# Attention and triangular inverse as one matrix per system in a five-stage ViT kernel on one core

## The chip, the cores and the metric

One core of a Trainium2 chip runs the whole forward pass in one launch. The metric is device microseconds of that core from start to end, the median of three runs. Engines: TensorE (PE; PEld is its weight load), VectorE (DVE), ScalarE (ACT), GpSimd (POOL), and SyncE (SP), which issues DMAs.

## The reference

Input is 64 images of 3 x 96 x 96; each becomes TOK = 37 tokens of D = 256. Five stages follow, each added to its input: embedding, 16-head attention with shared keys, a gated mixture of low rank (MuMoE), a delta-rule attention with two heads of 128, and a top-1 expert network with 8 experts. The change is in the fourth. For 37 tokens there is one chunk and a zero starting state, so per image and head it comes to:

```python
k = x / max(norm(x), 1e-12)                    # x: normalised rows, per head
v = (x @ W_write.T) * beta                     # beta = sigmoid(x @ W_beta.T)
A0 = tril(-((k * beta) @ k.T * L), -1)         # L[i, j] = gamma ** (i - j), i >= j
A = solve_triangular(eye - A0, eye, lower=True, unit_diagonal=True)
attn = tril(k @ k.T * L)
o = attn @ (A @ v)
return out + o @ W_read.T                      # both heads side by side
```

## The kernel before

All data is f32. Three images make a tile of R = 111 rows; there are NT = 22 tiles, PAIRS = 11 pairs of them. The work is in phases with barriers: embedding and first attention (to about 280 us), the gates, and a third phase (from 306 us) with MuMoE, the delta-rule attention, the router and the experts. Each engine runs its own list of instructions strictly in order, ordered among engines by semaphores with waits written by hand (`wait_ge`; `free(eng, sem, n)` waits for a buffer).

**Pair loop** (i from -1 to PAIRS + 1, about 306 to 455 us). Per pair: MuMoE, layer norm to `xn`, transposes to `xk`, then per tile `row_products` on TensorE (values and beta logits to bank 6, the Gram matrix of each head to bank 7). VectorE's `decay_products` makes two 111x222 products of the Gram matrix: with `lt` to `attn_t` (decayed lower part, transposed, kept for all tiles) and with `ln` to `nf`. GpSimd does `power_rows` (which the loop's next normalisation waits for), `add_rows` (h += xn), `inverses` (1/norm from the squares), `strengths` (four small operations per tile: beta, beta/norm, beta/norm^2, and beta/norm spread over the image mask) and `fold` (three images' blocks side by side to 37 columns per head, times the strength: rows of N). SP stores these rows to `n_rows` in DRAM.

**Solve.** Systems are regrouped, one system (image, head) per partition. Three GROUPS of pairs: 0 (tiles 0-9), 1 (10-15), 2 (16-21, LAST). SP's `load_systems(g)` brings N of a group; VectorE's `substitution(g)` solves for columns of the inverse X, two rows per step, as a generator: `advance(budget)` runs some steps in slots between VectorE's other work, by estimated costs. A group has SETS of partitions that share the columns, so X has 703, 481 and 370 values per partition in groups 0, 1 and 2. `identity_columns(g)` writes the identity there first. At the end an `engine_nop` signals `solved[g]`; SP's `store_inverses(g)` and `load_inverses(g)` bring X back by rows, in a round trip through DRAM.

**Tile loop** (t from 2 to NT + 4, about 455 to 531 us). A software pipeline; per turn:

- TensorE: `solve_values(t)` (ab x values, two heads), `read_out(t-1)` (each head to its own half of a bank), `turn_outputs(t-5)` (two transposes), `attend(t)`, `router_logits(t-5)`.
- ScalarE: `normalise_outputs(t-4)`, `copy_solved(t)`, `copy_turned(t-5)`, `scale_first(t-1)` (first head's read-out times 1/norm, to `first_half`), `copy_attended(t)`.
- VectorE: `add_read(t-2)` (second head's read-out times 1/norm, added to h; statistics; variance + EPS), `keep_logits(t-5)`, then `advance(1.1)`. Before tile 10 and tile 16 it must finish the substitution of their group (`advance(math.inf, ...)`).
- GpSimd (its own t from 0): `add_first(t-1)` (h += first_half), `spread_inverses(t+2)` (inverse blocks to the 111x222 matrix `ab`), `power_outputs(t-2)` (1/std).

Then `route` counts tokens per expert on VectorE, with placing matmuls on TensorE (L1011) and filler matmuls before and behind them (`keep_busy`, L992 to 995). After that come 26 tiles of 128 rows through their experts. SP loads `in_w` in three parts (L1343, L1346, L998); the last waits for all stores of `x_rows`.

## Time and profile before

| | us |
|---|---|
| median of three runs | 780.35 |
| the three runs | 780.12, 780.35, 784.51 |
| the profiled execution | 781.44 |
| its span, first to last instruction | 779.7 |

| engine | busy us | share |
|---|---|---|
| TensorE | 672.8 | 86% |
| its weight loads | 512.7 | 66% |
| VectorE | 419.7 | 54% |
| GpSimd | 292.6 | 38% |
| ScalarE | 246.8 | 32% |

Busy is the time inside instructions, not the rate at which they work. Shares are means over stages with different limits; the stage from about 430 to 560 us is the one in which TensorE has holes. A granted clock of 1.00 is TensorE's full clock (2.4 GHz), 0.50 its lower one (1.2 GHz). "Idle before <- X" in a row means that the engine had nothing to do until X finished.

### The profile page before, as it was taken

The page shows a single profiled execution, that of the slowest core. Times are in us where ns is not written, and L with a number is a line of the kernel's source. Part 1 is how long each engine was busy: PE and PEld are TensorE (multiplying, and loading weights), DVE is VectorE, ACT ScalarE, POOL GpSimd, SP SyncE. Part 2 cuts the span into 40 slices and gives each one's busy share as a digit, 9 for nine tenths or more (in the row PEclk, how much of TensorE's full clock was granted, in tenths as well). Part 3 has the DMA queues.
Part 4 walks back from the last instruction along what each step waited for, and adds up shares of the span by engine and source line. Part 5 has one row for each costly group of instructions (what it writes and reads, how often), then busy time and mean ns, then how long its engine had stood idle before and what let it go on. Part 6 is the DMA issues. An engine that isn't in the chain of part 4 may idle for free.

```text
span 779.7 us, 13703 instructions
## 1 busy us (share of the span) xinstructions
PE 672.8 (86%) x4576; PEld 512.7 (66%) x4576; DVE 419.7 (54%) x1120; ACT 246.8 (32%) x679; POOL 292.6 (38%) x483
## 2 busy tenths in 40 slices
PE   5899999999997614999999589495999999999994
PEld 3566776676765413899999567373667676676763
DVE  2456677777665475244389999557233333333331
ACT  0123333333333114344444256261032323222231
POOL 2344544544444100165566777360222222223220
PEclk9899999999998755899999999896799999999998
DMA  8311001111100000000011216698101111211110
GB/s 302 123 36 32 24 21 34 37 36 37 37 2 1 1 0 2 1 6 8 22 24 32 43 45 236 254 362 309 54 28 55 44 59 41 62 41 51 53 34 14
DMA packets 25070, 50.73 MB, mean 65 GB/s; under 512 B 15611, under 2 KB 15741, under 8 KB 24363
## 3 DMA queue, kind: packets, MB, share of 16 engines
q1 hardware_dynamic: 21387, 35.36, 14.1%
q0 software_dynamic: 3328, 10.23, 4.3%
q10 hardware_dynamic: 288, 4.27, 1.3%
q8 instruction: 39, 0.64, 0.3%
q14 instruction: 28, 0.23, 0.1%
HBM read 39.99 MB, written 9.86 MB: 64 GB/s over the span
## 4 chain that ended last, share of the span: by engine, by line
PE 45%; DVE 7%; issue 4%; POOL 3%; ACT 0%; POOLq 0%; DVEq 0%; ACTq 0%
PE psum L1192 12%; PE psum L1168 11%; PE psum L1389 5%; PE psum L1401 4%; PE psum L1181 3%; PE psum L1435 2%; DVE work L1741 1%; PE psum L1369 1%; PE psum L1011 1%; DVE arena_w L1748 1%; PE psum L1379 1%; POOL work L1900 1%; PE psum L1411 1%; PE psum L1441 1%; POOL work L1889 1%
## 5 line engine op out<-in xcount | busy, mean ns | idle before, releaser
L1265 ACT ACTIVATE work<-psum,cst 128x128 f32<-128x128 f32 x208 | 56.6, 383 | 144.1 <-PE psum L1181 144.1
L1168 PE MATMUL psum<-arena_w,work 128*128 x208 | 93.7, 593 | 1.3 <-DVE work L1219 1.3
L1192 PE MATMUL psum<-arena_w,work 128*128 x416 | 94.2, 379 | 0.4 <-ACT work L1265 0.4
L1130 POOL DMA_INDIRECT out<-work,row_i x26 | 25.8, 990 | 158.0 <-DVE work L1241 158.0
L1192 PEld LDWEIGHTS psum<-arena_w,work 128*128 128x128 f32 x416 | 77.1, 190 | 10.5 <-issue 1.1
L1228 DVE COPY work<-psum 128x512 f32<-128x512 f32 x52 | 36.0, 692 | 67.7 <-PE psum L1168 57.4
L347 PE MATMUL psum<-arena_w 128*111 128x256 f32 x264 | 64.3, 397 | 4.9 <-DMA arena_w<-in_pack 4.9
L712 POOL TENSOR_TENSOR arena_w<-arena_w,work 101x592 f32<-101x592 f32 x33 | 39.6, 1200 | 71.8 <-DVE work L578 71.8
L1168 PEld LDWEIGHTS psum<-arena_w,work 128*128 128x128 f32 x208 | 37.5, 190 | 38.8 <-issue 38.8
L347 PEld LDWEIGHTS psum<-arena_w 128*111 128x111 f32 x264 | 46.8, 183 | 19.6 <-issue 9.6
L703 POOL TENSOR_TENSOR arena_w<-arena_w 128x296 f32<-128x296 f32 x66 | 44.0, 690 | 20.7 <-DVE arena_w L546 20.7
L1235 DVE TENSOR_TENSOR tokens<-psum,cst 128x256 f32<-128x256 f32 x26 | 11.1, 425 | 73.9 <-PE psum L1192 73.9
L401 PE MATMUL psum<-arena_w 128*37 128x296 f32 x264 | 41.2, 434 | 3.3 <-ACT arena_w L666 3.3
L635 ACT COPY arena_w<-psum 37x592 f32<-37x592 f32 x33 | 25.2, 765 | 57.8 <-PE psum L412 57.8
L1389 PE MATMUL psum<-arena_w 128*128 128x222 f32 x176 | 40.9, 379 | 0.5 <-DVE arena_w L1642 0.5
L1123 POOL DMA_INDIRECT tokens<-x_rows,row_i x26 | 25.5, 980 | 34.1 <-DVE gate_s L1086 26.5
L558 DVE TENSOR_REDUCE work<-psum 101x16 f32<-101x592 f32 x33 | 25.4, 771 | 23.8 <-PE psum L401 23.8
L1389 PEld LDWEIGHTS psum<-arena_w 128*128 128x128 f32 x176 | 34.3, 202 | 5.1 <-issue 3.0
L412 PEld LDWEIGHTS psum<-cst,arena_w 101*128 101x128 f32 x264 | 26.5, 149 | 16.6 <-POOL arena_w L712 9.0
L433 PE MATMUL psum<-arena_w 37*32 37x74 f32 x1056 | 24.5, 230 | 13.6 <-DVE arena_w L569 12.1
L1401 PE MATMUL psum<-arena_w 128*128 128x222 f32 x176 | 35.8, 356 | 0.0
L627 ACT ACTIVATE arena_w<-arena_w 101x592 f32<-101x592 f32 x33 | 23.5, 711 | 37.4 <-DVE arena_w L561 36.4
(220 smaller groups left out, 1332.4 us busy)
## 6 DMA issues: line engine op xcount, KB each, us to landing
arena_w<-in_w SPq DMA_DIRECT2D x2, 4096.0 KB, 13.6
arena_w<-in_x SPq DMA_DIRECT2D x22, 333.0 KB, 3.0
x_rows<-tokens SPq DMA_DIRECT2D x22, 192.0 KB, 5.2
arena_w<-in_pack ACTq DMA_DIRECT2D x1, 2442.0 KB, 9.2
cst<-in_packc ACTq DMA_DIRECT2D x1, 1727.0 KB, 13.4
arena_w<-in_pack SPq DMA_DIRECT2D x1, 818.5 KB, 7.0
arena_w<-in_pack SPq DMA_DIRECT2D x2, 384.0 KB, 4.3
arena_w<-n_rows SPq DMA_DIRECT2D x8, 85.6 KB, 2.8
```

Source lines behind the costliest of these rows:

```text
L347: mm = nc.tensor.matmul(bank[0][0:R, j * D:(j + 1) * D], xp[j][:, k * R:(k + 1) * R], w_lin[:, k, :], start=(k == 0), stop=(k == PC - 1))
L401: mm = nc.tensor.matmul(bank[4 + f][e * HP:e * HP + TOK, 0:HH * TOK], qt[:, a:a + TOK], kb[p % 2 * 2 + e], start=True, stop=True)
L412: mm = nc.tensor.transpose(turns_bank[:, c * 128:c * 128 + PR], prob[p % 2][:, c * 128:(c + 1) * 128], ident[0:PR, 0:PR])
L703: nc.gpsimd.tensor_tensor(kb[p % 2 * 2 + e].rearrange("p (h s) -> p h s", h=HH), kt[:, a:a + TOK].unsqueeze(1).broadcast_to([128, HH, TOK] ...
L712: nc.gpsimd.tensor_tensor(by_head(prob[p % 2], HP), by_head(prob[p % 2], HP), small[p % 2][:, 2 * NH:3 * NH].unsqueeze(2).broadcast_to([PR ...
L1130: pool.indirect_dma_start(out_h, bass.IndirectOffsetOnAxis(ap=row_i[:, 2 * i + j:2 * i + j + 1], axis=0), yo[j], None).then_inc(y_stored[j ...
L1168: mm = nc.tensor.matmul(bank[2 * j + f][:, :], xgt[j][:, k * 128:(k + 1) * 128], arena_w1[:, bass.ds(expert * (2 * FF) + (k * FF + f * 512 ...
L1192: mm = nc.tensor.matmul(bank[7][:, 0:D], ht[j][:, g * 128:(g + 1) * 128], arena_w2[:, bass.ds(expert * (FC * D) + g * D, D)], start=(g == ...
L1228: nc.vector.tensor_copy(hp[j][:, f * 512:(f + 1) * 512], bank[2 * j + f][:, :]).then_inc(h_out[j], 1)
L1265: nc.scalar.activation(ht[j][:, g * 128:(g + 1) * 128], bank[4 + f][:, k * 128:(k + 1) * 128], ACT.Gelu, bias=cst[:, bass.ds(expert * FC + ...
L1389: mm = nc.tensor.matmul(bank[2 + f // 2 % 2][:, (f % 2) * W:(f % 2 + 1) * W], w_out1[:, f, :], z1, start=True, stop=True)
L1401: mm = nc.tensor.matmul(bank[1][:, 0:W], w_in2[:, f, :], hid[:, f * W:(f + 1) * W], start=(f == 0), stop=(f == OC - 1))
```

## The change

With M = I - A0, A = M^-1, B = diag(beta) and D the diagonal of k k^T, attn = D + B^-1 (M - I), because M's part below the diagonal is beta times that of attn. Hence attn A B = D A B + I - B^-1 A B: below the diagonal entry (i, j) is A[i, j] times a factor of row i and one of column j, and the diagonal has a factor of its own. Applied to X in the solver's layout, one elementwise product gives the matrix that maps values to outputs. In the code:

- `attn_t`, `lt`, and their set-up (two ScalarE exponentials, two GpSimd products, two constants) go; `decay_products` makes one product.
- Rows of N are stored without strength, and grow from 37 to NW = 40 columns: the three further ones carry strength, the diagonal's correction and 1/norm. `factors(i)` on GpSimd computes these for a pair in ten small operations, in place of `strengths`; `fold` has two operations. A store of N now waits for `factors_ready` too. GpSimd's order in the pair loop changes: `fold(i-2, 0)`, `power_rows`, (`scale_columns`), `factors`, `add_rows`, `fold(i-2, 1)`, ..., (`last_factors`).
- In the solver's layout GpSimd scales N's columns (`scale_columns(g)`: a copy of 37 values, products of 324 and 648 values per partition) and builds the factor matrix F (`last_factors(g)`: two operations of X's size). `substitution(g)` waits for `scaled[g]` instead of the load, and ends with a product X F of X's size instead of the nop. For group 2 the two stand in GpSimd's tile loop, at t = 2 behind `spread_inverses(4)` and ahead of `power_outputs(0)`, and at t = 4.
- `identity_columns` writes two matrices, at i = 0, 1, 2 of the pair loop. Group 2 has room of its own, so its load no longer waits for `z1_done`.
- `solve_values`, `copy_solved`, `scale_first`, `add_first` go. `attend` multiplies the values with the new `ab` (norm factors in place of beta/norm) into banks 0 and 1; `read_out` sums both heads in one bank (2 or 3); transposes and logits use banks 4 and 5. `add_read` is one addition; + EPS moves to GpSimd's `power_outputs`. `keep_logits` moves to ScalarE as a copy; b_r is added once in `route`.
- Orders in a turn: TensorE `attend(t)`, `turn_outputs(t-5)`, `read_out(t-1)`, `router_logits(t-5)`; ScalarE `copy_attended(t)`, `copy_turned(t-5)`, `normalise_outputs(t-4)`, `keep_logits(t-5)`.
- `keep_busy` before the placing goes from 4 to 5 calls, over five banks.

```diff
@@ store_systems
                     sp.wait_ge(nk_ready, t + 1)
+                    sp.wait_ge(factors_ready, 3 * (t // 2 + 1))
@@ route_products, route
-                keep_busy(pe, 4)
+                keep_busy(pe, 5)
...
+                link(tt(by_tile(lgr), by_tile(lgr), c("b_r", R).unsqueeze(1).broadcast_to([R, NT, NE]), ALU.add))
@@ TensorE
-                def solve_values(t):
...
                 def attend(t):
...
-                    pe.wait_ge(vn_out, t + 1)
+                    pe.wait_ge(a_block, t + 1)
                     free(pe, o_out, t - 1)
                     for h in range(H1):
-                        a = (t * H1 + h) * R
-                        mm = nc.tensor.matmul(bank[2 + t % 2][:, h * R:(h + 1) * R], vn[t % 2][:, h * 128:(h + 1) * 128],
-                                              attn_t[:, a:a + R], start=True, stop=True)
+                        mm = nc.tensor.matmul(bank[t % 2][:, h * R:(h + 1) * R], x_half(t)[:, h * 128:(h + 1) * 128],
+                                              ab[t % 2][:, h * R:(h + 1) * R], start=True, stop=True)
...
-                        mm = nc.tensor.matmul(bank[4 + t % 2][0:R, h * D:(h + 1) * D], ot[t % 2][:, h * R:(h + 1) * R],
-                                              w_read[:, h, :], start=True, stop=True)
+                        mm = nc.tensor.matmul(bank[2 + t % 2][0:R, 0:D], ot[t % 2][:, h * R:(h + 1) * R],
+                                              w_read[:, h, :], start=(h == 0), stop=(h == H1 - 1))
...
                 for t in range(2, NT + 5):
-                    solve_values(t)
+                    attend(t)
+                    turn_outputs(t - 5)
                     read_out(t - 1)
-                    turn_outputs(t - 5)
-                    attend(t)
                     router_logits(t - 5)
@@ VectorE
-                    nc.vector.tensor_tensor(attn_t[:, t * H1 * R:(t + 1) * H1 * R], bank[7][0:R, 0:H1 * R], lt, ALU.mult)
...
-                    dve.wait_ge(n_in[g], 16 * H1 * sets)
+                    dve.wait_ge(scaled[g], 2)
...
-                    nc.vector.engine_nop().then_inc(solved[g], 1)
+                    dve.wait_ge(factored[g], 2)
+                    nc.vector.tensor_tensor(rows_x[0:used, :], rows_x[0:used, :], rows_f[0:used, :], ALU.mult).then_inc(solved[g], 1)
...
-                    nc.vector.scalar_tensor_tensor(h, bank[4 + j][0:R, D:2 * D], inv_all[:, t * H1 + 1:t * H1 + 2], h,
-                                                   ALU.mult, ALU.add).then_inc(added, 1)
+                    nc.vector.tensor_tensor(h, h, bank[2 + j][0:R, 0:D], ALU.add).then_inc(added, 1)
@@ GpSimd
+                def scale_columns(g):
...
+                    pool.wait_ge(n_in[g], 16 * H1 * SETS[g])
+                    ts(col_s[g][0:used, :], n[:, :, TOK], 1.0, None, ALU.mult).then_inc(col_ready[g], 1)
+                    pool.wait_ge(col_ready[g], 1)
+                    half = TOK // 2
+                    for r0, r1 in ((1, half + 1), (half + 1, TOK)):
+                        part = n[:, r0:r1, 0:r1 - 1]
+                        tt(part, part, col_s[g][0:used, 0:r1 - 1].unsqueeze(1).broadcast_to([used, r1 - r0, r1 - 1]),
+                           ALU.mult).then_inc(scaled[g], 1)
+
+                def last_factors(g):
...
+                    pool.wait_ge(zeroed[g], 2)
+                    for k, op in ((TOK + 2, ALU.mult), (TOK + 1, ALU.add)):
+                        tt(to, to, n[:, :, k].unsqueeze(1).broadcast_to(shape), op).then_inc(factored[g], 1)
...
                 for t in range(NT + 2):
-                    add_first(t - 1)
                     spread_inverses(t + 2)
+                    if t == 2:
+                        scale_columns(LAST)
                     power_outputs(t - 2)
+                    if t == 4:
+                        last_factors(LAST)
```

## Rows read from the trace of the kernel before

**Rows 1.** Stretches of the span: length, busy us (instructions) per engine, granted clock, DMA

```profile
390.00:410.00 20.00, 20.00 (x113) 18.26 (x112) 17.34 (x50) 9.72 (x35) 13.95 (x34) 1.00 0.10 22
430.00:450.00 20.00, 12.03 (x60) 10.01 (x59) 19.11 (x57) 6.16 (x27) 13.49 (x30) 0.86 0.29 40
480.00:490.00 10.00, 10.00 (x72) 8.48 (x70) 9.59 (x41) 7.03 (x20) 8.47 (x16) 1.00 1.07 461
```

**Rows 2.** Waits of SP's queue, 430 to 560 us: total, times, longest

```profile
SPq L1318 <- DVEq L1754: 35.7, 3, 21.3
```

**Rows 3.** Timeline of SP: start us, us, instruction

```profile
458.06 4.59 SPq L1300 DMA_DIRECT2D arena_w<-n_rows  x8
...
497.78 3.67 SPq L1318 DMA_DIRECT2D a_rows<-arena_w  x8
502.80 2.66 SPq L1324 DMA_DIRECT2D arena_w<-a_rows  x6
...
534.73 0.35 SPq L998 DMA_DIRECT2D arena_w<-in_w  x1
```

**Rows 4.** Timeline of TensorE, restart at tile 16 and one tile of the drain

```profile
505.59 1.20 PE L1450 MATMUL psum<-tokens,work 111*111 111x128 f32 x4 [11.11 <-POOL work L1889]
...
509.74 0.67 PE L1450 MATMUL psum<-tokens,work 111*111 111x128 f32 x4
...
517.45 0.67 PE L1450 MATMUL psum<-tokens,work 111*111 111x128 f32 x4
517.96 1.03 PE L1471 MATMUL psum<-cst,work 128*111 128x256 f32 x4
518.83 0.36 PE L1484 MATMUL psum<-cst,tokens 111*128 111x111 f32 x2
519.02 0.61 PE L1461 MATMUL psum<-arena_w,work 111*128 111x111 f32 x4
519.62 0.56 PE L1493 MATMUL psum<-cst,work 128*111 128x8 f32 x4
```

**Rows 5.** Timeline of VectorE

```profile
444.02 1.03 DVE L1741 TENSOR_TENSOR work<-arena_w 108x130 f32<-108x130 f32 x1
...
445.40 0.39 DVE L1741 TENSOR_TENSOR work<-arena_w 108x150 f32<-108x150 f32 x1
...
469.95 0.48 DVE L1775 SCALAR_TENSOR_TENSOR tokens<-psum,arena_w,tokens 111x256 f32<-111x256 f32 x1
...
493.58 0.47 DVE L1775 SCALAR_TENSOR_TENSOR tokens<-psum,arena_w,tokens 111x256 f32<-111x256 f32 x1
...
531.38 0.34 DVE L1027 TENSOR_REDUCE work<-work 111x22 f32<-111x176 f32 x1
```

**Rows 6.** Groups by line and form: count, busy us, mean ns of one, idle before

```profile
L1846 POOL TENSOR_TENSOR tokens<-tokens,arena_w 111x512 f32<-111x512 f32 x11 | 13.5, 1228 | 0.9 <-DVE arena_w L1678 0.9
L1864 POOL TENSOR_TENSOR arena_w<-arena_w 111x2 f32<-111x2 f32 x22 | 4.6, 208 | 1.8
L1698 DVE TENSOR_TENSOR arena_w<-cst,arena_w 120x703 f32<-120x703 f32 x1 | 0.9, 893 | 1.1 <-PEq L179 1.1
L1235 DVE TENSOR_TENSOR tokens<-psum,cst 128x256 f32<-128x256 f32 x26 | 11.1, 425 | 73.9 <-PE psum L1192 73.9
L1588 ACT COPY work<-psum 128x222 f32<-128x222 f32 x22 | 7.5, 343 | 17.0 <-PE psum L1484 17.0
```

**Rows 7.** Timeline of GpSimd, the first `power_outputs`

```profile
459.46 0.83 POOL L1900 TENSOR_TENSOR work<-work 111x1 f32<-111x1 f32 x1
```

**Rows 8.** Stretches and TensorE's timeline around the router's placing matmuls

```profile
542.00:544.00 2.00, 0.00 (x0) 0.00 (x0) 1.97 (x4) 0.00 (x0) 0.00 (x0) 0.86 1.18 508
544.00:546.00 2.00, 1.71 (x8) 1.71 (x9) 2.00 (x5) 0.00 (x0) 0.00 (x0) 0.50 0.64 279
...
535.26 5.96 PE L995 MATMUL psum<-cst 128*128 128x512 f32 x8
544.29 9.63 PE L1011 MATMUL psum<-tokens 111*128 111x52 f32 x44 [3.07 <-DVE tokens L1075]
```

## Blind prediction

> **What bounds the kernel now.** I read the table of stretches first, then the waits of the sync engine's queue (SP), then the timelines of SP, TensorE, VectorE and GpSimd from 430 to 560 us. Until about 430 us TensorE is busy in every microsecond at the full clock, 2.4 GHz [rows 1]: the third phase's pair loop is TensorE's, and what the change takes from VectorE or adds to GpSimd there is covered, as long as neither falls behind. From 430 us TensorE has holes. What is then waited for is the triangular solve on VectorE: SP waited 35.7 us, in three waits, for the end of a substitution before it could send the inverses away [rows 2]. The third (group 2) ends at about 497.7, its inverses are issued from 497.78, read back from 502.80 [rows 3], and TensorE, idle for 11.1 us, restarts at 505.59 [rows 4]. From there to the router's first instruction at 531.38 [rows 5] the last tiles drain at TensorE's rate, 2.57 us per tile [rows 4]. So the change pays in two places: (a) when substitution 2 ends, (b) how long the drain lasts. The expert stage behind is untouched.
>
> **(a) The end of substitution 2.** *In the loop.* Each tile loses the 111x222 product for attn_t; the neighbouring one on VectorE is of its form, and I count 0.3 us, two per pair, covered by TensorE until pair 10. `strengths` (4 small GpSimd operations per tile) becomes `factors` (10 per pair), `fold` loses one operation. A small one costs 0.21 us and about 0.07 of handover [rows 6], so GpSimd's work per pair is 14 operations before and after. Order matters more: at i = 11 the eight-operation difference falls badly, since all ten of `factors` (2.8 us at most, 2.4 by my count, as some are not chained) now stand before `add_rows` and `spread_inverses(0)`, where four stood: +1.4, minus 0.4 for `fold`, so a_block(0) comes 1.0 us later. `attend(0)` is ahead of `row_products(10, ...)` on TensorE, so the last rows of N move by that 1.0. At i = 12 `factors(10)` stands before `fold(10, 1)` again, and the store of tile 20 now waits for `factors_ready`, so its two DMAs come right before tile 21's: +0.5. The load of group 2, issued from 458.06 to 462.65 [rows 3], moves by 1.5.
>
> *New in front of the substitution.* `scale_columns(2)` on GpSimd: a strided copy of 37 values, a product of 324 and one of 648. GpSimd takes 1.23 us for 512 in two inputs [rows 6], so 0.3 + 0.8 + 1.4 = 2.5 us. The last load ends its issue at 462.65 + 1.5; with 1.6 us to land, my allowance, and the 2.5 that gives about 468.2. VectorE comes there itself at: before, add_read(4) was at 469.95 after 1.9 us of substitution setup, so setup began near 468.0 [rows 5]. Now VectorE is 1.1 us later into this stretch, has the product of X and F of group 1 (481 values, 0.65 us; 703 cost 0.89 [rows 6]) more to do, and is about 0.26 us shorter in each of four `add_read`s: 468.6. The two meet; the scaling costs nothing in itself here, but 2.5 us if VectorE had been early.
>
> *What waits behind it.* GpSimd is in order: behind `scale_columns(2)` stand `power_outputs(0)`, which before ran at 459.46 [rows 7], and `spread_inverses(5)`. ScalarE's `normalise_outputs(0)` waits for the first, TensorE's `attend(5)` for the second. So the tile pipeline stops from tile 5 until about 470 us, TensorE idles some 8 us and restarts at the low clock (1.2 GHz), as it does after the hole before 505.59, where its four instructions of a solve take 1.20 us instead of 0.67 [rows 4]. Tile 4's `add_read` comes at about 473.3 where it was at 469.95 [rows 5]. VectorE is idle for those 3 us, since the substitution's next step stands behind that `add_read`. Two tiles more at a partly low clock, then VectorE sets the pace. Before, the nine tiles from `add_read(4)` to `add_read(13)` took 23.6 us [rows 5], 2.63 each, of which 1.33 was `add_read` with `keep_logits` and 1.30 substitution. Now the first is 1.07: the addition in 425 ns instead of 478 [rows 6], no EPS addition, no logits. Seven tiles gain 0.26 each, 1.8 in all, `add_read(13)` lands near 494.6, and the last steps plus the final product (0.5) end near 498.7: **+1.0 us**. Bounds: VectorE catches the stop up whole: -1.5; the stop is paid in full, from 459.46 to 468.2: +8.7.
>
> **(b) The drain.** The gaps between starts of one tile give TensorE's five parts [rows 4]: solve 0.51, read-out 0.87, turn 0.19, attend 0.60, logits 0.41. The solve goes; read-out keeps its two products, only accumulated. 2.57 becomes 2.06. Others per tile: ScalarE loses copy_solved and scale_first and gains a copy of 8 values, about 1.4 us; GpSimd loses `add_first` and gains a small operation, about 1.8; VectorE 1.07. All under 2.06. First tile at the low clock, 505.59 to 509.74 [rows 4]: 4.15 less its solve of 1.0: **-1.0**. Five more: 5 x 0.51 = **-2.55**. The rest, 509.74 + 5 x 2.57 = 522.6 to 531.38, is 8.8 us. Now: one iteration of 0.19 + 0.87 + 0.41 = 1.5, then four where only turn, a 0.34 us copy of 128x222 on ScalarE [rows 6] and logits alternate, 0.2 + 0.34 + 0.41 and three handovers, about 1.2 each, and 0.5 for the last logits and their copy: 6.9, **-1.9**. Sum **-5.4**; bounds -2.6 (only the five solves) and -7. The router gets b_r as one chained 111x176 addition: **+0.4**.
>
> **The router's filler.** `keep_busy` before the placing products goes from 4 to 5. Before, TensorE was idle from 541.2 to 544.29, the granted clock averaged 0.86 from 542 to 544 and was 0.50 after, so it fell shortly before the placing began; the 44 placing matmuls then ran at 0.50, 9.63 us for all [rows 8]. Four fillers took 5.96 us [rows 8], 1.5 each over both clocks; one more takes up to 1.5 us, about half of that if the clock has risen by then, so a quarter to half of that hole, so the clock may still be up when the placing starts. But those matmuls, 9.6 us without a hole, never raised it [rows 8]; I take them to lose it again soon. Bounds: 0 (clock already down) and half of 9.63, 4.8. I take nearer the first: **-1.3**. The last expert weights, issued 534.73 [rows 3], move with the issue of the stores, +1, and stay ahead of the experts' start near 560.
>
> **Sum.** +1.0 - 5.4 + 0.4 - 1.3 = -5.3 us. Against the profiled execution's own 781.44 (span 779.7, 1.7 around it) that is 776.1. That execution lay 1.1 above the median of 780.35; from the median it is 775.0.
>
> The locked port: VectorE's product of 130 values took 1.03 us beside GpSimd's 512-value addition, one of 150 alone 0.39 [rows 5]. The Trainium skill, "SBUF — State Buffer", section "Who interferes with whom", says that a VectorE operation with two SBUF inputs is shut out for a whole GpSimd instruction that reads SBUF, the exclusive lock going to whoever starts first. By that rule, which the row bears out, the new large GpSimd operations (three scalings, six factor products) speak against the change.
>
> **Rivals.**
> 1. *The placing keeps the full clock.* The shorter hole speaks for it, the 0.50 throughout the placing against. Price 4.8 instead of 1.3: **771.5**. Chance 0.17.
> 2. *The drain doesn't go at TensorE's pace.* ScalarE's `keep_logits` of one tile now stands before `copy_attended` of the next, so a ring TensorE-ScalarE-TensorE could hold 2.57. Then only the first tile and the drain gain, 2.9 instead of 5.4: **777.5**. ScalarE's idle share speaks against. Chance 0.12.
> 3. *The stop behind `scale_columns(2)` is paid in full* (slower). Place: GpSimd's third turn of the tile loop. 8.7 instead of 1.0: **782.7**. It decides once substitution 2 ends over 6.3 us later than before, 504. For it: GpSimd, ScalarE and TensorE stop together, and VectorE advances only behind an `add_read`. Against: VectorE's 0.26 per tile and TensorE's 0.51. Chance 0.12.
> 4. *Large GpSimd operations shut VectorE out*: each of `last_factors(2)` (370 values, 0.8 us twice) and four collisions of 0.6 us, as in rows 5, on VectorE's path in this stretch: +3.5: **778.5**. The Trainium skill's rule quoted above would have it so. Chance 0.12.
>
> **Chances.** The forecast 0.47, its own range 773 to 777.5. 775.0 is its time. The range 770.5 to 781 takes in rivals 1, 2 and 4. Within 1% (772.5 to 788.2) is about what a measurement of this kernel can't tell from no change: the forecast and rivals 2, 3 and 4 lie there, with an eighth of the forecast below it. Faster by over 1%: rival 1 and that eighth, 0.23. Slower by over 1% only if 3 and 4 join: 0.06. Same: 0.71.
>
> **What would show it.** The issue of group 2's inverses: 498.8 (was 497.78). VectorE idle about 3 us before tile 4's addition, and GpSimd waiting for the load of n_rows: the stop. Starts of one line on TensorE 2.06 us apart in the drain. From TensorE's restart to the router's first instruction 20.4 us (was 25.8). The granted clock in the placing: above 0.50 in its first microseconds. Wrong it goes if the issue comes later than 504, if the spacing stays at 2.57, or if the placing takes 5 us. The loop to 425 us should be the same to 0.5 us.

## Result: 2.5% slower, and the profile after

| | before | after |
|---|---|---|
| median of the paired runs | 781.21 us | 802.69 us |
| ratio, 95% interval | | 1.0253 [1.0213, 1.0293] |
| profiled execution (span, mean granted clock) | 781.44 (779.7, 0.925) | 802.33 (800.5, 0.900) |
| first power of the pair loop (GpSimd) | 324.48 | 322.59 |
| load of group 2 issued | 458.06 | 467.73 |
| inverses of group 2 stored | 497.78 | 511.45 |
| TensorE restarts at tile 16 | 505.59 | 521.04 |
| router's first instruction | 531.38 | 551.88 |
| placing begins | 544.29 | 565.17 |

Ratios leave out runs more than 1.5% above the fastest of their kernel; where single runs are told below, all of them are. The table splits the 20.5 us by which the router starts late: 13.7 up to the store of the last inverses, 1.8 more until TensorE restarts (9.6 us from store to restart, 7.8 before), and 5.0 in the drain, 30.8 us where it was 25.8. I had predicted +1.0 for the first and -5.4 for the last.

Positions in the span can't be compared more finely than by 4 us as they stand: in the twenty profiles of this document the pair loop's first power comes anywhere from 321.0 to 324.8 us, for kernels that are the same up to there too. Counted from that power, the last store is 15.6 us late after (188.9 us; before 173.3) and the load of group 2 11.6 us (145.1; 133.6). Where it matters, times below are counted so.

Of the 1.8 us between store and restart, the way of the inverses through DRAM has all: 6.9 us from the issue of the last store to that of the load behind it, where before took 5.0. SP sends a part of the expert weights (`in_w`) right behind group 1's inverses, now 18.7 us ahead of the last store, before 21.7. From 510 to 512 us, as the last store goes out, the DMA still moves 528 GB/s; in the kernel before it moved 33 from 496 to 498. In the other profiles the step takes 7.6 us where the weights go out 17.3 us ahead of the store and 5.0 where it is 20.4 (`e_slots`, `e_group_dve`). That one causes the other is argued from this alone.

SP's timeline after (start us, us, instruction), beside [rows 3]:

```profile
467.73 3.55 SPq L1293 DMA_DIRECT2D arena_w<-n_rows  x8
484.59 2.41 SPq L1311 DMA_DIRECT2D a_rows<-arena_w  x6
...
511.45 3.63 SPq L1311 DMA_DIRECT2D a_rows<-arena_w  x8
518.30 2.66 SPq L1317 DMA_DIRECT2D arena_w<-a_rows  x6
```

Turn 7 of the pair loop, after: first GpSimd, then VectorE.

```profile
402.61 4.24 POOL L1866 TENSOR_TENSOR arena_w<-arena_w 120x703 f32<-120x703 f32 x2
406.81 0.31 POOL L1842 TENSOR_TENSOR arena_w<-arena_w 111x74 f32<-111x74 f32 x1
407.20 0.32 POOL L1843 TENSOR_TENSOR arena_w<-arena_w 111x74 f32<-111x74 f32 x1
407.48 0.72 POOL L1789 TENSOR_TENSOR arena_w<-arena_w,work 111x2 f32<-111x2 f32 x1
```

```profile
404.07 0.59 DVE L1632 TENSOR_SCALAR arena_w<-arena_w 111x2 f32<-111x2 f32 x1
...
408.23 0.74 DVE L1643 TENSOR_SCALAR arena_w<-tokens,arena_w 111x256 f32<-111x256 f32 x2 [2.83 <-POOL arena_w L1789]
```

`last_factors(0)` (L1866) holds GpSimd for 4.24 us. The variance that `power_rows` (L1789) waits for was there at 404.66 (L1632 above: 404.07 and 0.59), and it runs at 407.48. VectorE's `normalise` and with it the whole pair wait 2.83 us. TensorE, busy for all of 390 to 410 us before [rows 1], now has a hole:

```profile
400.00:410.00 10.00, 7.99 (x44) 6.72 (x43) 7.00 (x21) 4.56 (x16) 9.26 (x16) 1.00 0.04 8
```

In turn 10 it is worse: GpSimd first waits for the load of N, then scales, and makes F:

```profile
434.92 0.37 POOL L1850 TENSOR_SCALAR arena_w<-arena_w 108x37 f32<-108x37 f32 x1 [3.36 <-DMA arena_w<-n_rows]
435.37 3.05 POOL L1855 TENSOR_TENSOR arena_w<-arena_w 108x324 f32<-108x324 f32 x2
...
445.27 2.96 POOL L1866 TENSOR_TENSOR arena_w<-arena_w 108x481 f32<-108x481 f32 x2
...
448.84 0.72 POOL L1789 TENSOR_TENSOR arena_w<-arena_w,work 111x2 f32<-111x2 f32 x1
```

The power of the last pair came at 441.98 before and comes at 448.84. From one power to the next, turn 7 takes 15.9 us (before 11.7) and turn 10 18.9 (12.7). Everything behind it (squares, factors, fold, store, load of group 2) moves with it. Among the tiles stands the stop that I had foreseen, but longer. GpSimd, ScalarE, VectorE in this order:

```profile
474.57 0.37 POOL L1850 TENSOR_SCALAR arena_w<-arena_w 128x37 f32<-128x37 f32 x1 [6.55 <-DMA arena_w<-n_rows]
```

```profile
478.83 0.60 ACT L1572 ACTIVATE tokens<-tokens,work 111x256 f32<-111x256 f32 x1 [7.47 <-POOL work L1889]
```

```profile
479.53 0.43 DVE L1741 BATCH_NORM_STATS2 work<-tokens 111x6 f32<-111x256 f32 x1 [7.52 <-ACT tokens L1572]
...
482.84 1.72 DVE L1718 TENSOR_TENSOR arena_w<-arena_w 108x481 f32<-108x481 f32 x1
484.49 0.82 DVE L1681 TENSOR_TENSOR work<-arena_w 128x648 f32<-128x648 f32 x1
485.34 1.66 DVE L1684 TENSOR_TENSOR arena_w<-arena_w,work 128x648 f32<-128x648 f32 x1
```

VectorE idles 7.5 us in front of the statistics (L1741), and behind them stood the last step of group 1's substitution. Group 2's begins at 484.49; I had 468.6. Last the drain on TensorE, one turn and the start of the next, and its stretches (length, busy us of PE, PEld, DVE, ACT, POOL, clock, DMA share, GB/s):

```profile
521.04 1.19 PE L1444 MATMUL psum<-work,tokens 111*128 111x111 f32 x4 [14.14 <-POOL work L1876]
522.03 0.58 PE L1467 MATMUL psum<-cst,tokens 111*128 111x111 f32 x2
522.40 1.92 PE L1454 MATMUL psum<-cst,work 128*111 128x256 f32 x4
524.11 0.78 PE L1476 MATMUL psum<-cst,work 128*111 128x8 f32 x4
524.74 1.17 PE L1444 MATMUL psum<-work,tokens 111*128 111x111 f32 x4
```

```profile
490.00:510.00 20.00, 15.63 (x109) 13.48 (x107) 19.21 (x76) 10.07 (x32) 11.74 (x30) 1.00 0.93 374
510.00:540.00 30.00, 18.96 (x72) 16.63 (x73) 6.71 (x20) 6.76 (x20) 10.37 (x26) 0.51 0.77 274
```

A tile takes 3.70 us at half clock (1.2 GHz); before it took 2.57 at full clock [rows 4]. From 530 to 540 us TensorE was busy in every microsecond and the granted clock stayed at 0.50.

### The profile page after: what moved, and what is told of

Read it like the earlier page. It is cut to its first block, busy times and chain, and to the rows that moved or that the text cites. A ratio compares the mean times of both kernels' runs of the same rounds, so it can differ in the third digit from the quotient of the medians.

```text
span 800.5 us, 13413 instructions
## 1 busy us (share of the span) xinstructions
PE 671.9 (84%) x4490; PEld 513.1 (64%) x4490; DVE 409.3 (51%) x1061; ACT 234.2 (29%) x655; POOL 303.4 (38%) x496
## 4 chain that ended last, share of the span: by engine, by line
PE 43%; POOL 6%; DVE 5%; issue 4%; DMA 2%; SPq 1%; ACT 0%; POOLq 0%; DVEq 0%; ACTq 0%
PE psum L1186 11%; PE psum L1162 11%; PE psum L1383 3%; PE psum L1175 3%; PE psum L1395 3%; PE psum L1454 2%; PE psum L1429 2%; PE psum L1004 1%; DVE work L1704 1%; PE psum L1363 1%; PE psum L1444 1%; DMA arena_w<-n_rows 1%; POOL arena_w L1866 1%; PE psum L1373 1%; PE psum L1476 1%
## 5 line engine op out<-in xcount | busy, mean ns | idle before, releaser
L1124 POOL DMA_INDIRECT out<-work,row_i x26 | 25.8, 990 | 158.0 <-DVE work L1235 158.0
L707 POOL TENSOR_TENSOR arena_w<-arena_w 128x296 f32<-128x296 f32 x66 | 44.1, 691 | 21.2 <-DVE arena_w L550 21.2
L1444 PE MATMUL psum<-work,tokens 111*128 111x111 f32 x88 | 19.8, 363 | 32.3 <-POOL work L1876 32.3
L1383 PE MATMUL psum<-arena_w 128*128 128x222 f32 x176 | 41.1, 379 | 0.5 <-DVE arena_w L1607 0.5
L1117 POOL DMA_INDIRECT tokens<-x_rows,row_i x26 | 25.5, 981 | 34.5 <-DVE gate_s L1080 26.9
L1444 PEld LDWEIGHTS psum<-work,tokens 111*128 111x128 f32 x88 | 16.4, 259 | 33.7 <-POOL work L1876 33.4
## 6 DMA issues: line engine op xcount, KB each, us to landing
x_rows<-tokens SPq DMA_DIRECT2D x22, 192.0 KB, 6.3
```

What stands on the lines that cost most here:

```text
L707: nc.gpsimd.tensor_tensor(kb[p % 2 * 2 + e].rearrange("p (h s) -> p h s", h=HH), kt[:, a:a + TOK].unsqueeze(1).broadcast_to([128, HH, TOK] ...
L1124: pool.indirect_dma_start(out_h, bass.IndirectOffsetOnAxis(ap=row_i[:, 2 * i + j:2 * i + j + 1], axis=0), yo[j], None).then_inc(y_stored[j ...
L1383: mm = nc.tensor.matmul(bank[2 + f // 2 % 2][:, (f % 2) * W:(f % 2 + 1) * W], w_out1[:, f, :], z1, start=True, stop=True)
L1444: mm = nc.tensor.matmul(bank[t % 2][:, h * R:(h + 1) * R], x_half(t)[:, h * 128:(h + 1) * 128], ab[t % 2][:, h * R:(h + 1) * R], start=Tru ...
```

## Experiments

Theories at the start: GpSimd's new work on the groups of systems delays the chain (in the pair loop by its length and order, among the tiles by its wait for the load); the statistics now wait for the normalisation of the tile before (`normed2` in place of `powered2`), an edit that I had overlooked; TensorE's clock is lost in the drain. "Load", "store" and "restart" are the three events of the table above. For the runs on which most rests, in us from the loop's first power, and last from TensorE's restart to the router's first instruction:

| | load of group 2 | store of group 1 | last store | restart | restart to router |
|---|---|---|---|---|---|
| before | 133.6 | 143.6 | 173.3 | 181.1 | 25.8 |
| after | 145.1 | 162.0 | 188.9 | 198.5 | 30.8 |
| `e_powered` | 145.2 | 160.5 | 188.1 | 196.8 | 25.8 |
| `e_group_dve` | 140.6 | 151.8 | 180.3 | 188.0 | 21.1 |
| `b_pool` | 139.1 | 149.4 | 179.2 | 186.9 | 27.0 |
| `b_thin` | 137.7 | 148.0 | 177.7 | 185.4 | 29.0 |
| `e_g01` | 140.6 | 159.9 | 188.9 | 196.9 | 25.8 |
| `e_g2` | 145.0 | 153.3 | 184.3 | 192.0 | 30.7 |
| `e_slots` | 145.1 | 158.3 | 183.8 | 198.3 | 21.2 |
| `b_front` | 131.5 | 145.9 | 173.1 | 182.1 | 25.0 |

(`e_slots` and `b_front` have no hole there; their "restart" is the start of tile 16.)

**One part at a time, against the changed kernel.**

`e_powered`, the statistics' wait put back:

```diff
-                    free(dve, normed2, t - 1)
+                    free(dve, powered2, t - 1)
                     nc.vector.bn_stats(st2[j][:, 0:6], h).then_inc(stat2, 1)
```

> The changed kernel, but VectorE's bn_stats waits for powered2 as before, not for normed2 (ScalarE's normalisation). Theory (the wait ties VectorE to ScalarE, which waits for GpSimd): the stop of 7.5 us behind tile 2's addition goes, substitution 1 ends at once, and substitution 2 starts when the scaled columns are there, 477.5 instead of 484.5; restart of TensorE at tile 16 about 514 instead of 521, time about 796. The drain's 3.68 us per tile stays, since TensorE itself is busy through it. Rival (the wait only shows what GpSimd's stop costs anyway): substitution 2 starts within 2 us of 484.5, time 801 to 803.

Measured 795.3 and 797.1 (ratio 1.020). Store of group 1 482.74 instead of 484.59, last store 510.33, restart 519.07; the clock rose after four tiles of the drain. The wait costs 1 to 2 us where it stands. Of the 7.1 us between the two profiled executions 5.1 lie in the drain, 25.8 us instead of 30.8, and are the clock. VectorE still stood for 7.16 us in the stop, now for GpSimd's power itself, and group 2's substitution began at 482.63: the rival's mark, though not its time.

`e_fill`, TensorE work without purpose, one product of 256 columns per turn from tile 5:

```diff
...
+                    if t >= 5:
+                        for k in range(1):
+                            nc.tensor.matmul(bank[6 + (t + k) % 2][:, 0:256], ident, cst[:, 0:256], start=True, stop=True)
                     router_logits(t - 5)
```

> The changed kernel with one filler matmul of 256 columns per turn of the tile loop from t = 5 on, ahead of the logits; it writes two banks that nothing reads. Theory (without the solve the drain doesn't raise the clock): the granted clock in the drain goes from 0.50 to 1.00 after the first tiles, the tile spacing from 3.68 to about 2.5 us, router 6 to 8 us earlier, time about 796. Rival (the spacing is a ring of waits among TensorE, ScalarE and VectorE): the clock stays, spacing 3.7 to 4.5, time 803 to 808.

Measured 799.0 and 791.5. Restart 523.13, tiles 4.55, 4.53, 2.70, then 2.32 us apart: the clock came back in the third. That is the theory's spacing at its end, but the time of the profiled run, 798.98, lies between the theory's 796 and the rival's 803.

`e_scale_dve`, the scaling of N on VectorE at the head of the substitution; GpSimd waits for the load only in `last_factors`:

```diff
-                    if i - 3 in ends:
-                        scale_columns(ends[i - 3])
...
+                        nc.vector.tensor_tensor(part, part, col_s[g][0:used, 0:r1 - 1].unsqueeze(1).broadcast_to(
+                            [used, r1 - r0, r1 - 1]), ALU.mult).then_inc(scaled[g], 1)
```

> The changed kernel, but the columns of N are scaled by VectorE at the head of each substitution (a copy of 37 values, products of 324 and 648, about 1.5 us per group); GpSimd keeps the factor matrix F. Theory (GpSimd, waiting in order for the load of N and scaling it, holds up the pair loop's power and fold): GpSimd's waits for the load of n_rows go (9.9 us in two), the issue of group 2's load comes at 459 to 462 instead of 467.7, substitution 2 starts 12 to 15 us earlier, time 789 to 793. Rival (it is the amount of GpSimd work, above all F's products at 4.2 and 3.0 us): the load's issue moves by less than 4 us, time above 796.

Measured 793.9 and 796.8. The stop is nearly gone (store of group 1 at 477.31), but the load stays at 468.82 (0.8 us earlier, counted from the first power): the scaling was not what made it late.

`e_all`, the three together:

> All three edits together on the changed kernel. If they are separate causes: substitution 2 starts near 470, ends near 497, the drain runs at 2.5 us per tile at full clock, time 778 to 783, about the kernel before. If one cause underlies the others, no better than the best single edit by more than 3 us.

Measured 790.9 and 791.2 (1.014 [1.005, 1.023]), between the two expectations. Store of group 1 477.39, as in `e_scale_dve`, but last store 510.53, 3.9 us later than there. Tiles 8 to 10 were 4.5 us apart at half clock, 3.7 without the filler: I take it that this took back what the earlier start gave; no run separates it.

**All work on groups off GpSimd.** `e_group_dve` also makes F on VectorE:

```diff
-                    if i - 3 in ends:
-                        last_factors(ends[i - 3])
...
+                    for k, op in ((TOK + 2, ALU.mult), (TOK + 1, ALU.add)):
+                        nc.vector.tensor_tensor(f, f, n[:, :, k].unsqueeze(1).broadcast_to([used, cols, TOK]), op
+                                                ).then_inc(factored[g], 1)
```

> All work on the groups of systems taken off GpSimd: the scaling of N's columns and the two products that make F run on VectorE, at the head of each substitution, behind its load; GpSimd keeps only the ten small factor instructions of each pair. Theory A (GpSimd's 2 x 2.1 us for F, standing in turns 7 and 10 ahead of the next pair's power, delay the pair loop): the load of group 2 is issued at 460 to 463 us, not 468.8 as with the scaling alone on VectorE, and the power of the tenth pair at 443 to 445 instead of 449.3; the time is 788 to 791. Rival B (the small factor instructions, ten where there were eight of two tiles, delay the last pairs): the load is issued at 467 to 469 as before and the time is 795 to 798, more by the 1.9 us that VectorE gets for each group.

Measured 783.4 median (1.0067 [1.0022, 1.0112]); five of eight runs 782.3 to 783.4 (mean clock 0.915), two 792.2 and 792.6 (0.903), one 797.3 (0.885). The power of the last pair comes at 444.44, as theory A says, the load at 464.57, between A's range and B's, the last store at 504.25. 18 of the 21 us go. The profiles split them: the last store comes 8.5 us earlier than after, and from restart to router it takes 21.1 us instead of 30.8. For the first half theory A stands. The second half is the clock in the drain, and that GpSimd's work decides it is not shown. The load is still 7.1 us late (from the first power): 3.2 are turns 7 and 10, where VectorE's setup is longer (`e_best` below), and 4.1 lie behind the last power, from where the load takes 20.1 us (before 16.1); `e_front` below tells what they are. The drain:

```profile
511.90 1.20 PE L1444 MATMUL psum<-work,tokens 111*128 111x111 f32 x4 [14.06 <-POOL work L1865]
...
515.43 0.68 PE L1444 MATMUL psum<-work,tokens 111*128 111x111 f32 x4
...
517.32 0.68 PE L1444 MATMUL psum<-work,tokens 111*128 111x111 f32 x4
```

One cold turn (at half clock) of 3.53 us and then 1.89 each: the same instructions as after, at the other clock. From restart to router 21.1 us.

**The same work added to the kernel before.** `b_pool` (two products of 703 values at the end of turns 7 and 10) and `b_thin` (one in each of turns 6, 7, 9, 10); nothing reads them. The edit of `b_pool`; `b_thin` has `(6, 7, 9, 10)` and the first product alone:

```diff
                     inverses(i - 1)
+                    if i in (7, 10):
+                        f = spare_f[0:120, :].rearrange("p (c i) -> p c i", c=19)
+                        lane = c("lane", 120)[:, 0:TOK].unsqueeze(1).broadcast_to([120, 19, TOK])
+                        link(tt(f, lane, lane, ALU.mult))
+                        link(tt(f, f, lane, ALU.add))
```

> The kernel before with two products of 703 values on 120 partitions added on GpSimd in turns 7 and 10, where the changed kernel makes F; nothing else is changed and nothing reads them. Theory A: the power of the next pair is 4 us late in each of the two turns, the load of group 2 is issued at 463 to 466 instead of 458.06, and since the end of the last substitution follows it the time is 784 to 788 against 780. Rival E (what the prediction held: work in those turns is covered or caught up): load at 458 to 459 and 779.5 to 781.

785.5, ratio 1.0070 [1.0045, 1.0095]: load at 463.89, store at 503.94. Added alone the work costs 5.4 us, and the load is 5.5 us late counted from the first power, although the products took only 1.36 to 2.02 us each and not 2.1. What the prediction held, that those turns cover it, is wrong. The two of turn 7:

```profile
400.72 1.36 POOL L1919 TENSOR_TENSOR arena_w<-cst 120x703 f32<-120x703 f32 x1
402.16 1.55 POOL L1920 TENSOR_TENSOR arena_w<-arena_w,cst 120x703 f32<-120x703 f32 x1
```

> The kernel before with the same four products of 703 values on GpSimd as in b_pool, but one in each of turns 6, 7, 9 and 10 instead of two in turns 7 and 10. Theory A1 (what counts is whether one turn's extra work is longer than GpSimd's idle time in that turn, 2.2 us ahead of the next fold plus 0.8 ahead of the power): each 2.1 us fits, the power of the tenth pair comes at 442 to 444, the load of group 2 at 458 to 460 and the time is 780 to 782. Rival A2 (what counts is the amount, wherever it stands, because GpSimd and VectorE slow each other): 784 to 787 as b_pool.

789.0, 1.0126 [1.0104, 1.0148], so A1 falls: spread out, the work is not covered either. It does cost a little less up to the last store (4.4 us late, `b_pool` 5.9); that the time is nevertheless longer is the drain, 29.0 us with two tiles at half clock, where `b_pool` had 27.0 with one. From one power to the next a turn grew by 1.5, 0.8 and 1.7 us in turns 7, 9 and 10, and by 0.0 in turn 6, the only one with no substitution on VectorE. GpSimd's product, and VectorE beside it:

```profile
398.78 1.36 POOL L1919 TENSOR_TENSOR arena_w<-cst 120x703 f32<-120x703 f32 x1
```

```profile
397.89 2.36 DVE L1742 TENSOR_TENSOR work<-arena_w 120x90 f32<-120x90 f32 x1
400.28 0.25 DVE L1749 TENSOR_REDUCE arena_w<-work 120x10 f32<-120x90 f32 x1
```

VectorE's product of 90 values takes 2.36 us and ends with GpSimd's, which starts 0.9 us after it behind another; in the kernel before the same one took 0.25:

```profile
399.54 0.25 DVE L1741 TENSOR_TENSOR work<-arena_w 120x90 f32<-120x90 f32 x1
```

So GpSimd's work costs twice: by its place in GpSimd's queue, and by holding VectorE.

**Half of the groups.** `e_g01` moves groups 0 and 1 to VectorE (its edit is shown), `e_g2` only group 2, with `(2,)`:

```diff
                 def last_factors(g):
+                    if g in (0, 1):
+                        return
```

(and the same in `scale_columns`, with VectorE's instructions of `e_group_dve` for these groups)

> The changed kernel with the group work of groups 0 and 1 on VectorE (turns 7 and 10 of the pair loop are free of it) and that of group 2 left on GpSimd among the first tiles. Theory A (the pair loop's two stretches are the larger part): the load of group 2 goes out at 464 to 465 as in e_group_dve, GpSimd then waits 4 to 5 us for it in tile 2, and the time is 786 to 790. Rival S (the stop among the tiles is the larger part of the 18 us): 792 to 797.

> The mirror of e_g01: groups 0 and 1 on GpSimd as in the changed kernel, group 2's scaling and F on VectorE, so that GpSimd waits for no load among the tiles. Theory A: the load of group 2 stays at 467 to 468, the wait of 6.55 us and VectorE's 7.5 us behind it are gone, substitution 1 ends at 477 to 479 instead of 484.6 and the time is 793 to 797. Rival S: 786 to 790. If the two halves are independent, their gains add up to the 18 us of both.

`e_g01` 799.3 (1.0246), load at 464.80 as foreseen, but store of group 1 at 484.06 and last store at 513.08. `e_g2` 796.7 (1.0190), load 468.59, store of group 1 476.88, last store 507.90. The halves give 3 and 6 us against 802.7, both 19: not additive. `e_g01` misses both of its ranges, `e_g2`'s time lies in theory A's (793 to 797). In `e_g01` GpSimd waits 6.88 us for the load and VectorE's stop among the tiles is as long as after (7.53 us); six tiles behind it ran at half clock, and the last store is where it was, 188.9 us from the first power: the load's 4.5 us are gone. And in both profiles the drain ran its first four to six tiles 3.68 us apart; `e_g2` took 30.7 us from restart to router where `e_group_dve` took 21.1. Nearly 10 us of the 19 are that one difference.

**VectorE's share for each tile.** `e_slots` changes one number of the changed kernel:

```diff
-SLOTS = (0.7, 0.8, 4.2, 1.1)
+SLOTS = (0.7, 0.8, 4.2, 2.2)
```

> The changed kernel with one number changed: VectorE hands out 2.2 instead of 1.1 us of substitution work for each tile. Theory K (at half clock a tile takes 3.68 us and VectorE gives group 2's substitution only 1.1 of them until tile 16, so a low clock in the tile loop delays the end of the substitution too): the last substitution takes 23 to 25 us instead of 26.9, its store goes out at 507 to 509 and the time is 796 to 799. Rival: VectorE was idle enough, or the tiles slow down by as much, and it stays at 800 to 803.

789.1, 1.0106 [1.0077, 1.0134], 14 us faster and more than theory K gave. Store of group 1 479.83, last store 505.32, 5.0 us earlier than after from the first power. But this earlier store is not what made the profiled run (791.4) faster. Its tiles ran at half clock, 3.68 us each from tile 8 on, and had not ended when the inverses came: there is no stop in TensorE's stream, and tile 16 starts 198.3 us from the first power, as after (198.5). The clock rose one tile later, and from tile 16 to the router it took 21.2 us instead of 30.8: that, and a loop that began 1.1 us earlier, is its gain. What a larger share is worth at the same clock this run doesn't show. That a low clock among the tiles slows the substitution (theory K) is seen in the next run.

**Where filler helps.** `e_fill_late`, in the changed kernel, five products of 512 columns ahead of tile 16's and two of 256 per turn from 17; `e_combo` is `e_group_dve` with the wait of `e_powered`, the same five, and one per turn:

```diff
                 for t in range(2, NT + 5):
+                    if t == 16:
...
+                        for k in range(5):
+                            nc.tensor.matmul(bank[6 + k % 2], ident, cst[:, 0:512], start=True, stop=True)
                     attend(t)
+                    if t >= 17:
+                        for k in range(2):
+                            nc.tensor.matmul(bank[6 + k % 2][:, 0:256], ident, cst[:, 0:256], start=True, stop=True)
```

> The changed kernel with TensorE kept at work without purpose: five products of 512 columns ahead of the head products of tile 16, in the stop while group 2's inverses travel, and two of 256 columns in each turn from 17 on. Theory C (the drain runs at half clock because TensorE has too little to do around the stop): the clock stays up or comes back within the first tile after the restart, tiles follow each other in 2.1 to 2.6 us instead of 3.68, and the time is 791 to 795 against 801. Rival D (the clock is down from before the stop, whatever fills it): spacing 3.7 to 4.5 for at least the first three tiles and 799 to 804.

805.5: the clock came back at the second tile of the drain, as C says (0.71 us for its four products instead of 1.17), but in this execution the tiles before ran at half clock and the last store went out at 522.06, 38.8 us after group 1's (26.9 in the kernel after, at full clock): with 1.1 us for each tile, tiles of 3.68 us slow the substitution. Each turn with its two products took 2.78 us, and from restart to router it took 28.9: where it brings back the clock, the filler costs most of that again. The time misses both ranges.

> Three repairs together: group work on VectorE, the wait ahead of the statistics put back on the power of the tile before (not on its normalisation), and filler products in the stop (five of 512 columns) and from turn 17 on (one of 256 columns). If theories A and C hold and the three do not share their gain: 801 minus about 10 (A with the wait) minus about 8 (C) gives 781 to 785, level with the kernel before. If either falls it stays at 788 to 792.

`e_combo` 787.4, 1.0097 [1.0067, 1.0128], four above `e_group_dve`: its filler ended 9.6 us before the restart and did not keep the clock, and each turn of the drain grew from 1.89 to 2.35 (restart to router 26.7 us). Its last store is where `e_group_dve` has it: the wait of `e_powered` is worth nothing here.

**Orders and setup.** `e_front` is `e_group_dve` with the products of tiles 0 and 1 behind the last rows of the pair loop; `e_front_y` adds 2.2 us for each tile, F's columns copied to a row, and the setup in two pieces; `b_front` is the same order and share in the kernel before.

```diff
-                    if i == PAIRS + 1:
-                        attend(0)
                     row_products(i - 2, 0)
...
                     turn_rows(i - 1)
+                attend(0)
+                attend(1)
+                read_out(0)
                 for t in range(2, NT + 5):
```

> The changed kernel with all group work on VectorE (as e_group_dve, 783.4), and the head products of tiles 0 and 1 with their copies and spreads put behind the last rows of the pair loop. What is left of the 20 us is then the 6.5 us by which the load of group 2 is still late (464.57 against 458.06), and theory H says that the last pair's squares, factors and fold wait there behind attend(0), whose matrix comes late: the load goes out 5 to 7 us earlier (457 to 460). The end follows only as far as VectorE is done with group 1 (475.0 in e_group_dve), so the time is 780 to 783. Rival: the load goes out earlier but VectorE's own queue ends group 1 at the same time and the time stays at 783 to 784.

> e_front with VectorE given a share of 2.2 instead of 1.1 us of substitution work for each tile, F's columns copied to a row of their own before the two products, and the setup handed out in two pieces. If VectorE's queue is what holds the end of group 1 (theory V), the substitution of group 1 ends 4 to 6 us earlier than in e_group_dve, the last store of the inverses goes out before 500 us instead of 504.25, and the time is 774 to 779, under the kernel before. Rival: tiles 0 to 15 are slowed by as much, and the time is 780 to 783.

> The kernel before with the same two changes of order: the first tiles' products behind the pair loop and 2.2 us of substitution work for each tile. If the two repairs have nothing to do with the identity they bring the kernel before the same 3 to 7 us: 773 to 777; then what the change itself is worth is read between this run and e_front_y. Rival: in the kernel before attend(0) holds nobody up (it comes at 446.6) and it stays within 1 us of 780.

`e_front`: 782.74, 784.75, 798.46, 798.81 (clocks 0.912, 0.906, 0.889, 0.889). The load went out at 460.16, 16.2 us behind the last power (20.1 in `e_group_dve`): theory H's cause is right, its 5 to 7 us were 4.4. In the kernel before the same order takes 14.0, so 2.2 us may still be the ten instructions of `factors` (rival B). The last store went out at 503.42 instead of 504.25: VectorE's queue held it (the rival). `e_front_y`: 780.7 to 791.0, median 786.8, over theory V's 774 to 779; load 458.15, last store 499.75 (before 500, as V says), then 6.8 us from store to load instead of 5.0. `b_front`: 780.2, 1.0022 [0.9995, 1.0050]. Its last store went out at 494.08, but its loop began 3.5 us early too: counted from the first power it is where it was (173.1 us; before 173.3), so orders and share gave nothing in the kernel before.

**Towards a version that is not slower.** `e_best`: `e_group_dve` with the statistics' wait on `powered2`, 1.8 us per tile, columns copied, setup in two pieces. `e_best_stop` adds six products of 512 columns ahead of tile 16, `e_best_turn` instead one of 256 per turn from tile 3. Against `e_group_dve`:

```diff
+                    yield 1.6
                     dve.wait_ge(scaled[g], 2)
...
-                        nc.vector.tensor_tensor(f, f, n[:, :, k].unsqueeze(1).broadcast_to([used, cols, TOK]), op
+                        nc.vector.tensor_tensor(f, f, col_s[g][0:used, (k - TOK) * TOK:(k - TOK + 1) * TOK].unsqueeze(1).broadcast_to([used, cols, TOK]), op
```

> The changed kernel with all group work on VectorE, F's columns copied to a row of their own first (2.25 ns a value read with a stride of 40 values would come down to 1.3), the setup handed out in two pieces, the statistics' wait back on the power, and 1.8 us of substitution for each tile; no filler. Sum: e_group_dve 783 minus 1 (columns) minus 1.6 in turn 7 and 1.6 in turn 10 (the setup in two pieces) minus 1 (wait) gives 778 to 780 when the drain runs at full clock; where it runs at half clock, 9 to 12 us more, as e_group_dve's single runs did (792 and 797 beside 783). Rival: 783 to 785, the rest is VectorE's own work, 3 us more for each group.

`e_best`: 778.35 in the profiled run (0.914), the other six 784.3 to 790.5 (0.897 to 0.903). The setup in pieces, with the columns copied, brought turns 7 and 10 back to 11.7 and 12.4 us (13.3 and 14.3 in `e_group_dve`; before 11.7 and 12.7).

> e_best with six products of 512 columns on TensorE in the stop ahead of tile 16 and nothing else. e_best's own runs were 778.35 at a mean clock of 0.914 and 784 to 790 at 0.897 to 0.903. Theory C2 (what the runs differ in is whether TensorE's clock stays up around the stop, and work in the stop decides it): the runs draw together at 778 to 781 and 0.914 to 0.92. Rival: the stop's filler changes nothing about it (the clock was decided among the tiles before) and the runs spread over 778 to 790 again.

> e_best with one product of 256 columns in each tile's turn from 3 on, about the TensorE work per tile that the change took away (0.43 us at full clock). Theory C3 (the shorter tile itself leaves TensorE too little work for its clock): the mean clock rises to 0.92, the drain keeps 2.3 us for each tile at full clock in all runs, and the time is 780 to 783 without a second group of runs. Rival: as e_fill and e_combo showed for the changed kernel, the filler lengthens the tiles (by 0.45 at full clock, 0.9 at half) and gives 784 to 790.

`e_best_stop`: 778.7, twelve runs from 776.7 to 782.1, ratio 0.9992 [0.9975, 1.0010]. `e_best_turn`: 781.1, twelve runs from 778.7 to 783.9, 1.0012 [0.9997, 1.0027]. The second group of runs is gone in both. C3 stands with its clock (0.916 to 0.921); of C2 the times drew together as it says, at a clock of 0.908 to 0.912, under its 0.914 to 0.920. TensorE around the restart of `e_best_stop`:

```profile
504.12 5.40 PE L1500 MATMUL psum<-cst 128*128 128x512 f32 x12
510.00 0.70 PE L1444 MATMUL psum<-work,tokens 111*128 111x111 f32 x4 [0.48 <-POOL work L1874]
...
511.91 0.68 PE L1444 MATMUL psum<-work,tokens 111*128 111x111 f32 x4
```

The filler ends half a microsecond before the restart, and the first tile is already at full clock (0.70 us, at half clock 1.19). The clock had risen with the filler's start: it averaged 0.50 from 503 to 504 us and 0.94 from 504 to 505. Restart to router: 18.5 us, the shortest of all. In that same execution the tiles before had run at half clock with TensorE busy throughout:

```profile
480.00:500.00 20.00, 20.00 (x76) 17.20 (x75) 18.58 (x71) 7.55 (x22) 9.35 (x23) 0.50 1.03 424
```

No version beats the kernel before by more than the measurement can tell.

## Why the prediction was wrong

1. **"What the change takes from VectorE or adds to GpSimd there is covered, as long as neither falls behind"; the loop to 425 us the same to 0.5 us.** This step failed first. I costed GpSimd's work in turn 11 and 12 and none of that in turns 7 and 10 (`scale_columns` and `last_factors` of groups 0 and 1). The power of the eighth pair came at 407.48 instead of 405.04, although the phase began 1.9 us earlier (first power 322.59 against 324.48), and that of the last 6.9 us late: 4.3 and 8.8 us counted from the first power. `b_pool` shows the price of F's work alone: 5.4 us. Behind the last power the load is another 2.8 us late, for which the prediction had 1.5. GpSimd's idle time in turn 7 before was 1.7 us ahead of `strengths` and 0.8 ahead of the power; work of 4.24 in a row doesn't fit in, and `power_rows` is on the loop's chain.
2. **"GpSimd takes 1.23 us for 512 in two inputs", so 0.8 for 370.** The size of a term: F's two products of 370 values took 3.42 us, of 703 values 4.24. They read a column with a stride of 40 values. Products of 703 without it took 1.36 and 1.55 us in turn 7 (`b_pool`) against 2.12. The Trainium skill, "GPSIMD Engine Reference", section "Performance pitfalls for Q7 kernels", says of such kernels that they pay about half more when a read of SBUF steps by more than 8 bytes; these rows of standard instructions agree (2.12 against 1.36 to 1.55), and I had not applied it. The stride is not all: per value the pair of 370 took half as long again as that of 703. It took 2.37 us in `e_slots` and 2.54 in `e_g01`, so about 1 of its 3.42 us is something else, most likely VectorE's products beside it.
3. **`scale_columns(2)` "costs nothing in itself": VectorE 468.6, scaled 468.2.** The rule of meeting was right, the load's time wrong: issued at 467.73, not 459.6, it landed 6.8 us after the issue began, 3.3 after it ended (my allowance was 1.6), and the scaling took 2.9 more. VectorE's stop was 7.5 us, not 3.
4. **The stop caught up by 0.26 us per tile.** I put only the substitution's next step behind `add_read(4)`. In the code bn_stats waits for `normed2` of the tile before, so VectorE stood still at 472, in the middle of group 1's substitution. By `e_powered` this wait costs 1 to 2 us; the load's lateness stopped VectorE for 7.16 us without it too.
5. **(b) The drain -5.4.** Right where the clock is up: 21.1 us from restart to router in `e_group_dve`, predicted 20.4, and 1.89 us for each tile, predicted 2.06. Wrong after, 30.8, because TensorE stayed at half clock for the six tiles. I had granted one cold tile, as before showed [rows 4].
6. **Filler and placing -1.3.** Zero: placing took 9.63 us as before. It is not fixed: it took 8.64 us in `e_best_turn`, 8.12 in `e_all`, 7.34 in `e_fill_late`, and 8.40 in `b_thin`, which has no filler of its own. None kept the full clock throughout, so rival 1 is false here.
7. **Rivals.** Rival 3 (the stop paid in full) had the sign and its mark, an issue later than 504: it came at 511.45. From the load to the store of group 1 it took 16.9 us where before took 10.0: most of these 6.8 is the stop. The 11.6 ahead of the load it doesn't have, and behind group 1's store 2.8 were caught up. Rival 4 (GpSimd holds VectorE) is shown by `b_thin` (2.36 us for 90 values; 0.25 alone) and by L1718 and L1684 in the profile after (1.72 us, 0.65 by my count; 1.66 us, the same form 0.83 in turn 7), but I had placed it at four collisions worth 3.5 us and not in the pair loop. The Trainium skill's rule quoted in the prediction ("SBUF — State Buffer", section "Who interferes with whom") agrees with these rows, and with turn 6 of `b_thin`, where VectorE had no product of two SBUF inputs beside it and nothing was lost. Rival 2 is false: no ring held 2.57.

What stays open: what decides the clock's level from one execution of a binary to the next. The runs show that it differs (`e_group_dve` 0.915, 0.903, 0.885), that it goes with 9 to 15 us, and that work on TensorE up to the restart, or in each turn, removes it; not why one execution keeps it. Nor does the length of the hole tell it: holes of 12.3 to 14.1 us were followed by one tile at half clock (`e_group_dve`), four (`e_powered`) or six (`e_scale_dve`, after). That in the slower runs of `e_group_dve` it is the drain that runs at half clock is inferred from the spans and clocks, as only the first was profiled.

## What to carry to other kernels

Cost a moved piece of work in every turn in which it occurs, and against the idle time in front of the next instruction that others wait for, not against the engine's idle share: GpSimd is 38% busy after, and 2.9 and 3.4 us more of it in two turns cost the kernel before 5.4. Where a chain passes from engine to engine, a wait for a transfer in an in-order queue stops all of them, so leave it with the engine that uses the data. When a change makes TensorE's work thinner around a hole, price it at both clocks and look whether work up to the end of the hole holds the clock. Count the events of two profiles from one that the change can't have moved, before an earlier time is called a gain.

## What the runs showed of the hardware

- A busy TensorE need not come back to full clock: 10.00 of 10 us busy at 0.50 after (530 to 540), and 20.00 of 20 in `e_best_stop`, both in the tiles' small products. With filler of 512 columns behind such a stretch it was back within the first microsecond (0.94 from 504 to 505 in `e_best_stop`, 1.00 from 520 in `e_fill_late`, whose filler began at 519.30).
- One cold turn or six: after the same kind of hole the drain of one stream of instructions took 21.1 us (`e_group_dve`) or 30.8 (after). The kernel before has it too: its drain took 25.8 us with one cold tile, 27.0 with one in `b_pool`, and 29.0 with two in `b_thin`.
- A broadcast column read with a stride of 40 values costs VectorE more than a packed row: two products of 370 values took 1.74 us, and 1.09 with the column copied to a row first (`e_best`), 2.35 against 1.47 ns a value.
- VectorE's product of 90 values took 2.36 us next to GpSimd's chain of products, ten times its 0.25.
